# Feed-forward products in reduced-precision halves, with the next stage's weights loaded later and its output weights scaled in eight pieces

## The reference, cut to what matters

```python
def _L0_ffn_ref(x, lut, gate_idx, up_idx, down_idx):   # INTER = 688, LUT_SIZE = 16
    def _ghost_linear(x, idx, lut):
        w = lut[idx]                                    # weights come from a table of 16 values
        return jnp.einsum('bsh,oh->bso', x, w)
    gate = _ghost_linear(x, gate_idx, lut)
    up = _ghost_linear(x, up_idx, lut)
    h = jax.nn.silu(gate) * up
    return _ghost_linear(h, down_idx, lut)

# layer 0
x = x + ga * _L0_attn_ref(h, ...)                       # 16 heads of 128
h = _layernorm(x, axis=-1) * (1 + cb) + sb
x = x + gb * _L0_ffn_ref(h, ...)
# layer 1: softmax attention, weights = codes * scales
h = _layernorm(x, axis=-1) * (1 + ca) + sa
q = h @ (wq_codes * wq_scales) + bq                     # k, v and, at the end, out @ (wo_codes * wo_scales) alike
x = x + ga * _L1_attn_ref(h, ...)
x = _L1_ffn_ref(...)                                    # 32 experts, 4 for each token
```

## Time and profile before

| | us |
|---|---|
| median of 3 runs | 1065.32 |
| lowest, highest | 1061.94, 1069.73 |
| profiled execution | 1066.8 |
| span of its profile | 1065.0 |
| PE busy | 998.2 (94%) |
| DVE busy | 776.8 (73%) |
| ACT busy | 580.1 (54%) |
| POOL busy | 288.9 (27%) |
| mean granted clock of PE | 0.966 of full |

### The profile page before, as it was taken

The page is one execution under the profiler, slowest core; times in us unless marked ns, Lnnn a source line. Parts: engine busy times, 40 slices in busy tenths (PEclk is TensorE's granted clock), DMA queues, the critical chain, the costliest instruction groups (busy, mean ns, idle before and its releaser), DMA issues.

```text
span 1065.0 us, 17345 instructions
## 1 busy us (share of the span) xinstructions
PE 998.2 (94%) x5864; PEld 796.6 (75%) x5864; DVE 776.8 (73%) x1351; ACT 580.1 (54%) x1153; POOL 288.9 (27%) x246
## 2 busy tenths in 40 slices
PE   7999999999999999999979999999997999659996
PEld 5778988898889854454459898989896545449995
DVE  4789999899989858983358777787877125638774
ACT  2567878887878687830136555555655012326651
POOL 1034234423442320130021212112110003536772
PEclk8999999999999999998989999999998999879998
DMA  7098777877876851160001101010100202547856
GB/s 230 2 234 169 175 161 156 171 170 155 167 164 159 243 111 49 70 177 0 1 32 58 58 31 59 30 59 30 59 0 1 74 1 95 220 147 226 246 163 212
DMA packets 82480, 121.59 MB, mean 114 GB/s; under 512 B 26099, under 2 KB 59646, under 8 KB 81792
## 3 DMA queue, kind: packets, MB, share of 16 engines
q1 hardware_dynamic: 70368, 86.88, 26.9%
q0 software_dynamic: 12032, 34.11, 16.2%
q10 hardware_dynamic: 32, 0.00, 0.0%
HBM read 70.28 MB, written 38.04 MB: 102 GB/s over the span
## 4 chain that ended last, share of the span: by engine, by line
PE 77%; DVE 11%; ACT 4%; issue 3%; DMA 3%; POOL 2%; POOLq 0%; ACTq 0%; DVEq 0%; SPq 0%
PE psum L690 11%; PE psum L691 11%; PE psum L692 11%; PE psum L916 5%; PE psum L1060 5%; PE psum L744 5%; PE psum L941 3%; PE psum L863 3%; PE psum L733 3%; PE psum L822 3%; PE psum L803 3%; PE psum L1113 2%; PE psum L872 2%; DVE arena L1580 2%; PE psum L668 1%
## 5 line engine op out<-in xcount | busy, mean ns | idle before, releaser
L1580 DVE SCALAR_TENSOR_TENSOR arena<-arena,par_in 128x1024 f32<-128x1024 f32 x144 | 183.4, 1283 | 32.7 <-ACT arena L1189 23.0
L690 PE MATMUL psum<-G_r,arena_r 128*128 128x512 f32 x320 | 132.8, 415 | 4.6 <-DVE G_r L1673 4.1
L691 PE MATMUL psum<-G_r,arena_r 128*128 128x512 f32 x320 | 128.0, 400 | 0.0
L692 PE MATMUL psum<-G_r,arena_r 128*128 128x512 f32 x320 | 127.7, 399 | 0.0
L690 PE MATMUL psum<-arena_r 128*128 128x256 f32 x384 | 117.8, 307 | 2.9 <-DVE arena_r L1763 1.5
L691 PE MATMUL psum<-arena_r 128*128 128x256 f32 x384 | 110.7, 288 | 0.0
L692 PE MATMUL psum<-arena_r 128*128 128x256 f32 x384 | 110.6, 288 | 0.0
L2040 POOL DMA_DIRECT2D arena<-arena x64 | 53.8, 983 | 206.8 <-DVE arena L1592 206.6
L1337 ACT ACTIVATE arena<-psum,small 128x256 f32<-128x256 f32 x128 | 59.3, 472 | 87.3 <-DVE small L1738 87.3
L1179 ACT ACTIVATE arena<-psum 128x1024 f32<-128x1024 f32 x48 | 49.3, 1026 | 62.2 <-PE psum L692 61.7
L2056 POOL TENSOR_TENSOR arena_r<-arena,arena_r 128x512 fp32r<-128x512 f32 x16 | 20.7, 1294 | 214.6 <-ACT arena_r L1306 214.6
(11 more groups left out here) (243 smaller groups left out, 2340.6 us busy)
## 6 DMA issues: line engine op xcount, KB each, us to landing
arena<-arena POOLq DMA_DIRECT2D x64, 256.0 KB, 5.7
slot_rows<-nowhere SPq DMA_DIRECT2D x16, 576.0 KB, 4.5
G<-in_w_moe SPq DMA_DIRECT2D x24, 384.0 KB, 8.9
arena<-slot_rows SPq DMA_DIRECT2D x32, 288.0 KB, 3.2
arena<-bands SPq DMA_DIRECT2D x16, 528.0 KB, 4.2
sq_rows<-arena POOLq DMA_DIRECT2D x16, 512.0 KB, 7.8
arena<-in_w_qkvz SPq DMA_DIRECT2D x16, 384.0 KB, 4.0
arena<-in_qkv_codes SPq DMA_DIRECT2D x16, 384.0 KB, 3.2
```

Of the source, the lines that this page charges most:

```text
L690: nc.tensor.matmul(dst, w_l, x_h, start=start, stop=False, skip_group_check=True)
L691: nc.tensor.matmul(dst, w_h, x_l, start=False, stop=False, skip_group_check=True)
L692: return nc.tensor.matmul(dst, w_h, x_h, start=False, stop=stop, skip_group_check=True)
L1580: nc.vector.scalar_tensor_tensor(by_batch(dst), by_batch(u[s])[:, :, j:j + S], par_in[:, bass.ds(M_CW + (w * H + h) * TAPS + j, 1)], by_ba ...
```

## The change

1. All feed-forward products but those of tiles m = 0, 1 in half n = 0 are made `by_halves`. ACT makes the upper parts: of x (`upper_x`), of the gate and up weights by tile (`upper_gate_up`), of the down weights in two parts (`upper_down`), and of each h tile (`upper_h`). DVE makes the lower ones (`lower_x`, `lower_gate_up`, `lower_down`, `lower_h`).
2. The look-up pieces 10 to 12, the squares of `n1b` and the splits stand in a new order on ACT and DVE. At the seam, x is split ahead of the weights (`upper_in(0)` ahead of `upper_w1(0, 0)`).
3. The upper parts lie where layer 1's weights lie later, so head 0's codes are loaded only when the last up product is made, and head 0's POOL work moves behind `n2a`. The codes and scales of layer 1's output weights (2 MB each) are loaded after `down(1)`.
4. The output weights' codes and scales were multiplied by one POOL instruction of 128x4096. Now eight of 128x512 stand in the loop over heads, each between `weights` and `weights_lower`, for heads 2 to 9.

The new semaphores share registers with older ones: in the rows of the order below, `a0_tap_q` is `f_w_hi`, `a0_rs_q` is `f_w_lo`, `a0_rs_k` is `f_x_hi`, `a0_on_lo` is `f_x_lo`, `a0_sq_k` is `f_h_hi`. `arena_s` and `G_s` are the rest of the buffers of `arena_r` and `G_r`.

```diff
 SP
-            sp.wait_ge(sg("a0_gT"), H)
-            load1(0)
             sp.wait_ge(sg("attn_out"), 2 * KC)
             sp.dma_start(wmod[1], a["wmod1"]).then_inc(again("in_wmod1")[0], 16)
+            sp.wait_ge(sg("f_u"), 2 * MT)
+            load1(0)
+            sp.wait_ge(sg("a1_wmul"), 1)
+            load1(1)
+            sp.wait_ge(sg("f_down"), 2 * KC)
             sp.dma_start(wo_c, a["wo_codes"]).then_inc(sg("in_wo"), 16)
...
-            with sp.Fori(1, H) as h:
+            with sp.Fori(2, H) as h:
 PE
             def gate_up(n, m):
                 r, s = min(P, INTER - m * P), n * MT + m
-                if s >= 2:
+                full = n == 0 and m in in_full
+                if s >= 2 and s != 3:
                     pe.wait_ge(sg("f_h"), s - 1)
+                if not full:
+                    pe.wait_ge(*at("f_x_lo", KC * (n + 1)))
+                    pe.wait_ge(*at("f_w_lo", f_w_hi_at(m)))
...
+                            i = by_halves(ffn_bank(n, m, up)[0:r, :], wg_h[:, w], lut_w_r[:, w], part(xf[n][0], k), part(xf[n][1], k),
+                                          k == 0, k == KC - 1)
             def down(n):
+                pe.wait_ge(*at("f_w_lo", MT - len(in_full) + 2))
...
-                    pe.wait_ge(sg("f_h"), n * MT + m + 1)
+                    pe.wait_ge(*at("f_h_lo", n * MT + m + 1))
...
+                        i = by_halves(bank(6 + o), wd_h[0:r, c], wd_l[0:r, c], hsb_h[m][0:r, :], hsb_l[0:r, m * 512:m * 512 + 512],
+                                      m == 0, m == MT - 1)
 ACT
+            def upper_gate_up(m):
+                act.wait_ge(sg("lut_done"), -(-2 * UPC // LC))
+                act.wait_ge(sg("a0_sq_rows"), 16 * H)
+                nc.scalar.activation(up_tile(wg_h, m), up_tile(lut_w, m), ACT.Copy).then_inc(sg("f_w_hi"), 1)
...
+            def upper_h(n, m):
+                r = min(P, INTER - m * P)
+                act.wait_ge(sg("f_h"), n * MT + m + 1)
+                nc.scalar.activation(hsb_h[m][0:r, :], hsb[0:r, m * 512:m * 512 + 512], ACT.Copy).then_inc(sg("f_h_hi"), 1)
...
+            upper_x(0)
+            upper_gate_up(2)
+            upper_gate_up(3)
+            lut_act(10)
             silu_f(0, 0)
+            upper_gate_up(4)
+            silu_f(0, 1)
+            upper_h(0, 0)
+            upper_gate_up(5)
+            part_square_act(act, "n1b", fc, fsq)
+            silu_f(0, 2)
+            upper_h(0, 1)
+            silu_f(0, 3)
             lut_act(11)
...
+            upper_in(0)
             upper_w1(0, 0)
-            upper_in(0)
 DVE
+            def lower_h(n, m):
+                r, c = min(P, INTER - m * P), slice(m * 512, m * 512 + 512)
+                dve.wait_ge(*at("f_h_hi", n * MT + m + 1))
+                nc.vector.tensor_tensor(hsb_l[0:r, c], hsb[0:r, c], hsb_h[m][0:r, :].bitcast(F32), ALU.subtract)\
+                    .then_inc(sg("f_h_lo"), 1)
...
             lut_dve(9)
+            lower_x(0)
+            attn_half(1)
+            lower_gate_up(2)
             lut_dve(10)
-            attn_half(1)
+            lower_gate_up(3)
             product_f(0, 0)
...
 POOL
-            weights(0, 0)
-            part_rstd_pool(pool, "n1b", 1)
-            pool.wait_ge(sg("in_wo"), 80)
-            nc.gpsimd.tensor_tensor(wo_c, wo_c, wo_s, ALU.mult).then_inc(sg("a1_womul"), 1)
-            part_rstd_pool(pool, "n2a", 0)
+            part_rstd_pool(pool, "n1b", 1)
+            part_rstd_pool(pool, "n2a", 0)
+            weights(0, 0)
             weights_lower(0, 0)
             part_rstd_pool(pool, "n2b", 1)
             weights(1, 1)
             weights_lower(1, 1)
-            with pool.Fori(1, H // 2) as i:
+            def weights_out(p):
+                c = bass.ds(p * 2 * D, 2 * D)
+                nc.gpsimd.tensor_tensor(wo_c[:, c], wo_c[:, c], wo_s[:, c], ALU.mult).then_inc(sg("a1_womul"), 1)
+
+            pool.wait_ge(sg("in_wo"), 80)
+            with pool.Fori(1, H // 4 + 1) as i:
+                for par in range(2):
+                    weights(2 * i + par, par)
+                    weights_out(2 * i + par - 2)
+                    weights_lower(2 * i + par, par)
+            with pool.Fori(H // 4 + 1, H // 2) as i:
```

More of the change, by code:

```diff
@@ L123, in sb, with twice @@
         return ctx.enter_context(nc.sbuf_tensor(name, [P, cols], dt))[:, :]
-    def twice(name, cols):
+    def twice(name, first, cols):
         with nc.sbuf_tensor(name, [P, cols], F32) as t:
             plain = t[:, :]
-        return plain, sb(name + "_r", cols, F32R)
+        return plain, sb(name + "_r", first, F32R), sb(name + "_s", cols - first, F32R)
     with ctx:
@@ L140, in build @@
         cst, par_in = sb("cst", C_ALL), sb("par_in", M_ALL)
-        G, halves = twice("G", H * T + LUTC)
-        lut_w, lut_w_r = G[:, H * T:H * T + LUTC], halves[:, H * T:H * T + LUTC]
+        G, halves, lut_w_r = twice("G", H * T, H * T + LUTC)
+        lut_w = G[:, H * T:H * T + LUTC]
         nowhere, nil = sb("nowhere", ROW), sb("nil", D)
@@ L179, in carve @@
             for n in sizes:
-                v.append(of[:, o:o + n])
+                if of is not arena:
+                    assert o + n <= UPPER or o >= UPPER
+                    v.append(arena_r[0][:, o:o + n] if o < UPPER else arena_r[1][:, o - UPPER:o - UPPER + n])
+                else:
+                    v.append(of[:, o:o + n])
                 o += n
@@ L209, in build @@
         rb, sq_in = swq, swk
+        (wg_h,) = carve(2 * UPC, base=UPPER, of=arena_r)
+        wd_h, wd_l = halves[:, 10 * T + 512:12 * T], lut_w_r[:, 2 * UPC:LUTC]
+        xf = [[halves[:, 0:T], halves[:, T:2 * T]], [halves[:, 2 * T:3 * T], halves[:, 3 * T:4 * T]]]
+        hsb_h = carve(*[512] * MT, base=at_w, of=arena_r)
+        (hsb_l,) = carve(MT * 512, base=3 * UW + 3 * T, of=arena_r)
+        in_full = (0, 1)
+        split_order = [m for m in range(MT) if m not in in_full] + list(in_full)
         (wout,) = carve(H * D, base=at_w)
@@ L1288, in _, with upper_x, upper_down @@
             part_square_act(act, "n1a", fc, fsq)
-            for c in range(7, 11):
-                lut_act(c)
+            lut_act(7)
+            lut_act(8)
+            lut_act(9)
+            def upper_x(n):
+                for k in range(KC):
+                    act.wait_ge(*norm(("n1a", "n1b")[n], "out", k))
+                    nc.scalar.activation(part(xf[n][0], k), half(h_t, k, n), ACT.Copy).then_inc(sg("f_x_hi"), 1)
+            def upper_gate_up(m):
+                act.wait_ge(sg("lut_done"), -(-2 * UPC // LC))
+                act.wait_ge(sg("a0_sq_rows"), 16 * H)
+                nc.scalar.activation(up_tile(wg_h, m), up_tile(lut_w, m), ACT.Copy).then_inc(sg("f_w_hi"), 1)
+            def upper_down():
+                act.wait_ge(sg("lut_done"), LCH)
+                act.wait_ge(sg("attn_out"), 2 * KC)
+                for j in range(2):
+                    nc.scalar.activation(down_part(wd_h, j), down_part(lut_w[:, 2 * UPC:LUTC], j), ACT.Copy).then_inc(sg("f_w_hi"), 1)
+            def upper_h(n, m):
+                r = min(P, INTER - m * P)
+                act.wait_ge(sg("f_h"), n * MT + m + 1)
[4 more added lines that the diff above has]
+            lut_act(10)
             def silu_f(n, m):
@@ L1308, in _ @@
             silu_f(0, 0)
+            upper_gate_up(4)
[6 more added lines that the diff above has]
+            silu_f(0, 3)
             lut_act(11)
-            silu_f(0, 1)
+            upper_h(0, 2)
+            silu_f(0, 4)
+            upper_h(0, 3)
             lut_act(12)
-            silu_f(0, 2)
-            part_square_act(act, "n1b", fc, fsq)
-            for m in range(3, MT):
-                silu_f(0, m)
-            for m in range(0, 3):
-                silu_f(1, m)
+            upper_down()
+            silu_f(0, 5)
+            upper_h(0, 4)
+            upper_h(0, 5)
+            upper_gate_up(0)
+            upper_gate_up(1)
+            upper_x(1)
+            silu_f(1, 0)
+            silu_f(1, 1)
+            upper_h(1, 0)
+            silu_f(1, 2)
+            upper_h(1, 1)
             part_square_act(act, "n2a", gc, gsq)
@@ L1674, in lower_in, with lower_x, lower_gate_up, lower_down @@
                         .then_inc(sg("in_lo"), 1)
+            def lower_x(n):
+                for k in range(KC):
+                    dve.wait_ge(*at("f_x_hi", KC * n + k + 1))
+                    nc.vector.tensor_tensor(part(xf[n][1], k), half(h_t, k, n), part(xf[n][0], k).bitcast(F32), ALU.subtract)\
+                        .then_inc(sg("f_x_lo"), 1)
+            def lower_gate_up(m):
+                dve.wait_ge(*at("f_w_hi", f_w_hi_at(m)))
+                if m in in_full:
+                    dve.wait_ge(sg("f_u"), m + 1)
+                nc.vector.tensor_tensor(up_tile(lut_w_r, m), up_tile(lut_w, m), up_tile(wg_h, m).bitcast(F32), ALU.subtract)\
+                    .then_inc(sg("f_w_lo"), 1)
+            def lower_down():
+                for j in range(2):
```

(5 more changed lines are left out.)

51 lines of the change are left out of this document (40 added, 11 removed), and 3 rows, old and new, of the table REUSED.

## The result

| | before | after |
|---|---|---|
| median of 15 runs each, on the same chips | 1065.84 us | 1060.89 us |
| lowest to highest | 1061.94 to 1069.88 | 1056.97 to 1063.66 |
| profiled execution, its own time | 1066.8 us | 1057.08 us |
| its span | 1065.0 us | 1055.3 us |

The ratio is 0.9947 with a 95% interval of 0.993 to 0.9964, that is 5.6 us less, between 3.8 and 7.5 (the two medians lie 5.0 apart). That is within the 1% that I called no change, though the interval leaves out zero. My forecast of 1062.0 us was a gain of 3.3.

The account below looks back on a forecast made before the run. PE was taken as the bound, with 77% of the chain that ended last. Terms of -10.1 us up to the seam and +6.8 us in the head loop gave -3.3 us, 1062.0 us against a median of 1065.3; range 1053.5 to 1068.

Parts of the forecast that it names:

- Products by halves: Feed-forward on PE: 40 gate and up products and 24 down products get cheaper, -10.7 us together.
- The stall before tile 2: First half of the feed-forward: PE waits there for DVE, which is still on look-up piece 10, about 2.0 us.
- The look-up holding `down(0)`: First down: DVE's look-up and splits let it start within a microsecond of PE's own pace, put at +0.3 us.
- POOL's product moved away: Before the feed-forward: a POOL product that slowed DVE's three selections moves away, so PE waits less, -0.9 us.
- The other wait of 0.96: PE's idle time before 459.63 us, which the new stall replaces, -1.0 us.
- Head 0's weights: Seam to layer 1: loading and POOL work after the last up product tie with PE's spread and down, +0.2 us.
- The half clock in `down(0)`: Part of the first down runs at half the granted clock after the tiny products; that loss of some 1.7 us stays.
- The loop: Layer 1's head loop: POOL's new products hold DVE's small softmax product, 7 x 0.8 + 1.2 = +6.8 us.
- The rival that the loop costs little: Head loop: POOL is late or DVE gets its turn, 1 to 2 us in all, 1055 to 1058 us; chance 0.22.
- The look-up rival: First down: DVE is 10 us late because ACT's interpolations stand behind silus, 1071 us; chance 0.09.
- the rival of products no cheaper: Feed-forward: a product by halves takes what a plain one takes, so the 10.7 us fall away, 1072.7 us; chance 0.03.
- every head pays the whole: Head loop: each of eight heads pays the whole new POOL product, 10.4 us, giving 1065.6 us, no change; chance 0.11.

Follow-up runs that it names:

- e3: The changed kernel with the down products plain again, without the splits of h and of the down weights; ratio to before 0.9962.
- e4: The changed kernel with tile 0's product on DVE ahead of look-up piece 10, and ACT's silu likewise; ratio to before 0.9919.
- e5: The changed kernel with the output weights' product as one POOL instruction of 128x4096 again, behind head 2's weights; ratio to before 1.0001.
- e6: The changed kernel with two POOL products of 128x256 in each of the eight heads instead of one of 128x512; ratio to before 0.994.
- e8: The kernel before, unchanged, profiled a second time; 1062.25 us for this one execution, span 1060.4 us.
- e2: The kernel before with only the output weights' product changed, from one of 128x4096 to eight of 128x512 in the head loop; ratio to before 1.0023.
- e1: The changed kernel with one more POOL wait, so each 128x512 product starts some 12 us later in its head; ratio to before 0.9916.
- e7: The changed kernel with both the later POOL products and tile 0's product ahead of look-up piece 10; median 1055.88 us, ratio to before 0.9912.

## Why the prediction was right

By its own steps, with the second profile of before as the fair partner for everything behind the small products:

- **Products by halves, -10.7:** right, as far as the profiles separate it. The six tiles of the second half with what lies between them came down by 4.15 us (3.9 forecast), the second `down` with its spread by 2.05 (2.1). e3 undid the `down` part alone and lost 3.4 of its 4.2.
- **The stall before tile 2, +2.0:** PE was ready at 448.81 + 1.72 = 450.53 and started at 452.24, so 1.7. e4 moved one product and the stall was gone, which shows its cause.
- **The look-up holding `down(0)`, +0.3:** no idle time of PE stands there. From the small products to the first tile of the second half the second profile of before and the one of after give 489.83 - 469.55 = 20.28 and 483.92 - 465.54 = 18.38. That is 1.9 less against a forecast of 1.8 (twelve down products, 2.1, less this 0.3).
- **POOL's product moved away, -0.9:** measured -0.86 at the first plain tile.
- **The other wait of 0.96, -1.0:** gone.
- **Head 0's weights, +0.2:** zero; POOL was ready 0.25 us ahead of PE. From the last up product to POOL's start it took 5.2 us (504.20 to 509.37), 4.9 in the forecast. The sum called it a tie; that it fell on the good side by a quarter of a microsecond is luck.
- **Sum up to the seam, -10.1:** measured -11.2 (134.6 to 123.4). The parts: small products 3.1 us sooner (2.5 forecast), from there to the projection 8.1 less (7.6). No single term that can be read is off by more than half a microsecond.
- **The half clock in `down(0)`:** I said that its loss stays. It does, but its length is not a constant of the kernel. With the first profile of before as partner, this adds 1.6 us to the gain, which I had no row to see. The forecast stood on that one profile.
- **The loop, +6.8:** measured +6.2, of which 0.4 is the alternation that is left open below. In the seven heads +0.8 each (17.90 against 17.10), as summed. In the first head I had put 1.2, and it is 0.1. That was the mis-sized term. DVE of the changed kernel there:

```profile
539.93 1.82 DVE L1869 TENSOR_SCALAR small<-small 128x2 f32<-128x2 f32 x1
541.66 0.68 DVE L1867 TENSOR_REDUCE small<-psum 128x2 f32<-128x512 f32 x1
542.37 0.63 DVE L1869 TENSOR_SCALAR small<-small 128x2 f32<-128x2 f32 x1
```

  POOL's `weights` ended at 541.73 and the new product ran from 541.68 to 542.98. The first small product ended at 541.75, not at 542.98. DVE does not wait across two POOL instructions: it gets its turn between them. The prediction wrote that no row shows such a wait, used it only for the rival, and still summed as if DVE waited across. In this head the second small product then paid 0.46 us instead of the first paying 1.3, and most of that was slack. In the other seven no small product is waiting when `weights` ends, so the rule changes nothing there.

The rival that the loop costs little named the turn between two instructions rightly, and drew from it that the heads pay 0.1 to 0.3 us. It fell because it needs DVE to be waiting already when POOL goes over; in seven heads of eight DVE comes 0.1 to 0.7 us after the new product has begun (612.37 against 612.02 in the head shown). Its other leg, that POOL is late by its register instructions, has no support: 612.02 is the end of `weights` at 612.07, with no gap. The look-up rival fell with the timeline of PE, the rival of products no cheaper with the 4.15 and 2.05 us of the second half and with e3, and "every head pays the whole" with the 17.90.

While e5's POOL product of 8.84 us ran, a DVE instruction between SBUF operands took 8.17 us, and one with its input in PSUM, which began at the turn of POOL's two instructions, took its usual 0.68. The Trainium skill's page GPSIMD Engine Reference, section 1 (Specifications), says that GpSimd's SBUF interfaces are shared with VectorE, with contention for DVE instructions in a 2-port mode or with two SBUF inputs. The 7.99 us of the earlier trace rows had two SBUF inputs and agrees. The small product has one tensor as input, so by that sentence it would have to be in a 2-port mode, which no row shows; that it is held, and to the end of the running instruction, comes from the rows.

The whole: forecast -3.3, measured -5.6 by the ratio (-5.0 between the medians), -6.0 in the traces from the common start, and -4.2 against the second profile of before, whose span ends 669.2 us from the start (671.0 in the first, 665.0 after). These differ by as much as the forecast missed. By its terms it is -11.2 + 6.2 = -5.0 against -10.1 + 6.8 = -3.3: both parts missed the same way, by 1.1 and 0.6 us, so the forecast did not come out by errors that cancel.

## What to carry to other kernels

Ask of each POOL product not how long it is but which DVE instruction with SBUF operands comes up while it runs, and whether that one has slack: eight products of 1.3 us cost 6.2 us at one place in the head and at most 1.0 at another. Cutting a product to pieces helps if a DVE instruction is let in between them (e6), and costs if each piece meets a chain without slack of its own (e5's big one cost 9.3 us once beyond before's first head, the eight cost 6.2, and before's place, under PE's small products, cost under 0.2 by the profiles of e8 and e2, though e2's run times leave room for more). Subtract two profiles from a step that both share and that lies just ahead of the change, and take a second profile of the old kernel before giving a name to the last two microseconds.

## What I had not expected of the hardware

- **How long DVE is held** when all its operands lie in SBUF: to the end of the POOL instruction that runs, and no further: 0.97 us beside one of 1.30, 8.17 beside one of 8.84, 0.42 beside two of 128x256. Between two POOL instructions without a gap DVE gets its turn (546.45 + 1.81 against 548.19 in e5; 539.93 + 1.82 against 541.68 in after).
- **The length of the half clock:** the same kernel spent 10.3 us at half in one execution and 6.8 in another, and its small products went from 7.97 to 6.06 us with it. In all three the fall came within these small products: 2.7 us after their start in the one (475.0 against 472.34), 4.8 in the other (474.4 against 469.55), 4.5 after (470.0 against 465.54).
- **The first attention:** its end moves by up to 10 us from execution to execution with unchanged code. Behind it the distances repeat to about 0.1 us where the granted clock is the same (78.36 and 78.35 us to the small products, 238.73 and 238.76 for the loop), and to 1 to 2 us where it isn't. I didn't look for its cause.
- **Left open:** in heads 10 and up the distances alternate between 17.11 and 17.23 us in the changed kernel (e1 and e4 to e7 too; in e1, e5 and e7, where no piece lengthens the heads, already from head 5 on, behind one of some 17.47), and are 17.10 throughout in before, e2 and e8. e3, with `down` plain, has none of it either. It is 0.4 us in all, and no run was made for it.
